# Two inverse square roots change engines in the feed-forward half: the output norm's goes to VectorE, the chain's first one to GpSimd

## The reference

```
def _layernorm(x, eps=1e-05): m = mean(x); v = var(x); return (x - m) / sqrt(v + eps)

def attn(x):                      # 16 heads of 64, softmax over 2048 keys
    ctx = softmax(q @ k.T / 8) @ v
    y = x + ctx @ Wo + bo
    return (y - mean(y)) * rsqrt(var(y) + 1e-3) * gamma + beta

def ffn(x):                       # 256 -> 768 -> 256, integer weights / 127
    return (silu(x @ wg.T) * (x @ wu.T)) @ wd.T

x = x + _layernorm(attn(_layernorm(x)))
x = x + _layernorm(ffn(_layernorm(x)))
```

## Time and profile before

| what | value |
|---|---|
| time, median of 3 runs | 2808.67 us (2808.62 to 2809.34) |
| the profiled execution's own time | 2810.7 us |
| its span | 2808.9 us |
| mean granted TensorE clock | 0.989 |
| busy share PE / DVE / ACT / POOL | 96% / 83% / 87% / 81% |
| feed-forward half | from about 2439 us to the end, some 370 us |
| one of turns 1 to 5 | 41.1 us, PE 38.8 busy, DVE 32.9, ACT 23.7, POOL 13.3 |

### The profile page before, as it was taken

One profiled execution on the slowest core, in us unless ns is written; L12 is line 12 of the kernel. 1 busy time (PEld: TensorE's weight loads), 2 busy tenths in 40 slices (PEclk: granted clock), 3 DMA queues, 4 the chain that ended last, 5 costly groups with the idle time before them and its releaser, 6 DMA issues. The chain is left out here.

```text
span 2808.9 us, 83179 instructions
## 1 busy us (share of the span) xinstructions
PE 2698.2 (96%) x34176; PEld 1727.5 (61%) x34176; DVE 2341.5 (83%) x4203; ACT 2447.0 (87%) x4760; POOL 2274.6 (81%) x1919
## 2 busy tenths in 40 slices
PE   5899999999999999899999999999999999989997
PEld 2466666666666666556666666666666666656764
DVE  4688888999998998768888889999999998678785
ACT  3799999999999999889999999999999999846553
POOL 3799999999989999789999899999999999613232
PEclk8999999999999999999999999999999999999998
DMA  3322123212211111122221222221111122321210
GB/s 101 75 56 53 40 52 75 45 41 41 41 36 39 36 40 40 39 81 58 54 46 44 53 53 41 41 42 41 41 40 40 37 42 70 99 76 46 91 53 23
DMA packets 207100, 144.89 MB, mean 52 GB/s; under 512 B 157824, under 2 KB 181632, under 8 KB 206720
## 3 DMA queue, kind: packets, MB, share of 16 engines
q1 hardware_dynamic: 206720, 139.58, 20.6%
HBM read 51.20 MB, written 37.88 MB: 32 GB/s over the span
## 5 line engine op out<-in xcount | busy, mean ns | idle before, releaser
L536 POOL TENSOR_TENSOR p_l<-p_f,p_h 128x512 f16<-128x512 f32 x1536 | 1946.2, 1295 | 92.9 <-ACT p_h L610 90.2
L663 DVE TENSOR_REDUCE mx<-ps_aux 128x1 f32<-128x512 f32 x2048 | 1349.5, 681 | 303.9 <-PE ps_aux L834 295.8
L609 ACT ACTIVATE p_f<-ps_score 128x512 f32<-128x512 f32 x2048 | 1271.7, 622 | 18.1 <-PE ps_score L863 17.9
L610 ACT ACTIVATE p_h<-ps_score 128x512 f16<-128x512 f32 x2048 | 1280.9, 627 | 0.0
L888 PEld LDWEIGHTS ps_ctx<-v_hi_one_lo,p_h 128*128 128x128 f16 x16384 | 891.4, 97 | 245.3 <-POOL p_l L536 1.2
L888 PE MATMUL ps_ctx<-v_hi_one_lo,p_h 128*128 128x65 f16 (+1 forms) x16384 | 920.8, 193 | 1.5 <-POOL p_l L536 0.9
L888 PE MATMUL ps_ctx<-v_hi_one_lo,p_l 128*128 128x65 f16 x8192 | 791.2, 192 | 0.0
L862 PE MATMUL ps_score<-q_hilo,k_hihi 128*128 128x512 f16 x2048 | 778.2, 380 | 7.4 <-ACT v_new L568 5.4
L863 PE MATMUL ps_score<-q_hi_max,k_lo_one 65*128 65x512 f16 x2048 | 780.1, 381 | 0.0
L834 PE MATMUL ps_aux<-k_hihi,q_hilo 128*128 128x512 f16 x2048 | 620.5, 382 | 21.7 <-DVE mx L663 13.7
L681 DVE TENSOR_TENSOR p_l<-p_f,p_h 128x512 f16<-128x512 f32 x512 | 536.3, 1048 | 22.6 <-ACT p_h L610 22.6
(11 more groups left out here) (174 smaller groups left out, 2163.4 us busy)
## 6 DMA issues: line engine op xcount, KB each, us to landing
v_heads<-v_new SPq DMA_DIRECT2D x64, 258.0 KB, 2.0
v_hi_one_lo<-v_heads SPq DMA_DIRECT2D x32, 516.0 KB, 6.0
heads<-ctx_n SPq DMA_DIRECT2D x128, 128.0 KB, 2.0
x_all<-heads SPq DMA_DIRECT2D x8, 2048.0 KB, 8.7
k_hihi<-hi_st SPq DMA_DIRECT2D x62, 256.0 KB, 4.4
q_hi_max<-hi_st SPq DMA_DIRECT2D x32, 256.0 KB, 3.6
k_lo_one<-lo_st SPq DMA_DIRECT2D x32, 256.0 KB, 4.3
q_hilo<-hi_st SPq DMA_DIRECT2D x31, 256.0 KB, 3.2
```

What stands on the lines that cost most here:

```text
L536: nc.gpsimd.tensor_tensor(p_l[:, r], p_f[:, r], p_h[:, r], ALU.subtract).then_inc(lo_pool, 1)
L609: nc.scalar.activation(p_f[:, r], ps_score[:, bank], ACT.Exp, scale=exp_scale)
L610: nc.scalar.activation(p_h[:, r], ps_score[:, bank], ACT.Exp, scale=exp_scale).then_inc(exp_done, 1)
L663: nc.vector.reduce_max(mx[:, blk % 2, tt, ch:ch + 1], ps_aux[:, n % SIDE], AX_X).then_inc(max_read, 1)
```

## The change

root_o moves from GpSimd, where it stood behind the first low part of the hidden slice, to VectorE, directly behind moments_o. The chain's first root moves from VectorE, where it stood behind f = 2, to GpSimd, behind the second low part (f = 1). Of this root the very first one, in the opening of the half, stays on VectorE. The root of the chain's second norm stays where it is.

```
@@ scalar
             def norm_chain(g, k, dst, src):
-                act.wait_ge(chain_root, (g * (NORMS - 1) + k) * SHIFT)
+                if k == 1:
+                    act.wait_ge(attended_root, SHIFT + g * POOL_ROOT)
+                else:
+                    act.wait_ge(chain_root, (g + 1) * SHIFT)
                 scaled(dst, src, small[3], shift, chain_normed)
...
             def norm_o(g):
-                act.wait_ge(o_root, (g + 1) * POOL_ROOT)
+                act.wait_ge(o_root, (g + 1) * SHIFT)
@@ gpsimd
-            def root_o(g):
-                pool.wait_ge(o_moments, (g + 1) * MOMENTS)
-                pool_root(nc, pool, small_o, shift_o, o_root, g * POOL_ROOT)
+            def root_attended(g):
+                pool.wait_ge(chain_moments, (g * 2 + 1) * MOMENTS)
+                pool_root(nc, pool, small, shift, attended_root, SHIFT + (g - 1) * POOL_ROOT)
...
-                    if f == 0 and g:
-                        root_o(g - 1)
+                    if f == 1 and chains(g):
+                        root_attended(g + 1)
@@ vector
             def root_chain(g, k):
-                root_here(small, shift, chain_root, (g * (NORMS - 1) + k - 1) * SHIFT)
+                if k == 1:
+                    root_here(small, shift, attended_root, 0)
+                else:
+                    root_here(small, shift, chain_root, g * SHIFT)
+
+            def root_o(g):
+                root_here(small_o, shift_o, o_root, g * SHIFT)
...
                     if f == 0 and g:
                         moments_o(g - 1)
+                        root_o(g - 1)
                     if f == 1 and chains(g):
                         moments_chain(g + 1, 1, z[1 - u])
-                    if f == 2 and chains(g):
-                        root_chain(g + 1, 1)
```

More of the change, by code:

```diff
@@ L1038, in feed_forward @@
         chain_moments = sem("chain_moments")
+        attended_root = sem("attended_root")
         chain_root = sem("chain_root")
```

## The result

| kernel | median | lowest to highest | runs |
|---|---|---|---|
| before | 2808.91 us | 2808.62 to 2810.75 | 5 |
| change | 2823.78 us | 2821.44 to 2825.46 | 5 |

The change makes the kernel slower: the ratio is 1.0051, with a 95% interval of 1.0037 to 1.0066, 14.9 us on the medians. The profiled execution has a span of 2822.0 us against 2808.9 us.

The account below looks back on a forecast made before the run. The end of the chain's root was taken to set each turn's end on PE. 5 x 2.4 + 1.4 + 1.8 + 0 = 15.2 us on 2810.7 gives 2825.9, less 2.0 for the median: 2823.9 us, range 2817 to 2829.

Parts of the forecast that it names:

- Step 1: On VectorE, root_o stands where hf 1 stood, is hit once by GpSimd's first hTl and costs 2.8 us.
- Steps 2 and 3: PE's transpose 3 waits for cTl 1, about 2 us late; ACT's hTh of f = 1 follows at 2627.03, before 2625.63.
- Step 4: GpSimd's hTl of f = 1 starts at 2627.74, its successor at 2628.86; the chain's statistics have a microsecond of slack.
- Step 5: GpSimd's fifteen root instructions take 4.26 us, so norm_attended starts 2.4 us later.
- Step 6: Everything behind norm_attended keeps its order and work, so each of turns 1 to 5 takes 2.4 us longer.
- Turn 0: No root_o here; the chain's root on GpSimd makes norm_attended 1.4 us later.
- Turn 6: An undisturbed root ahead of hf 1 makes norm_attended 1.8 us later, and PE waits for that chain's end.
- Turn 7: No chain here; its end hangs on the last hTl, so 0 was taken, with 1.85 us as upward bound.
- A: Rival: root_o isn't hit or hTl 1 isn't late; some 8 to 11 us in sum, 2818; chance 0.10.
- B: Rival: PE returns from its wait at transpose 3 at 1.2 GHz; 8 us more, 2832; chance 0.08.
- C: Rival: VectorE's list, not norm_attended, sets the turn's end; 9.3 us faster, 2799.4; chance 0.05.
- D: Rival: silu 4 isn't what hf 4 waited for, so no change within noise; 2810 to 2814; chance 0.05.

Follow-up runs that it names:

- e5: The change, with norm_attended moved on ACT from ahead of to behind the silu, high parts and hTh of f = 4: 2813.2 us.
- e6: The kernel before, with norm_attended moved behind f = 4 on ACT and the first residual behind the low parts of f = 5 on VectorE: 2801.8 us.
- e3: The change, with the output's root on VectorE moved from f = 0 to behind the low part of f = 3: 2817.0 us.
- e2: The change with root_o back on GpSimd behind f = 0, so only the chain's first root is moved: 2829.1 us.
- e9: The kernel before, with SyncE issuing the load of the next attention output ahead of the last residual's wait and store: 2809.0 us, ratio 0.9998.
- e1: The kernel before with only the output's root moved to VectorE behind its statistics: 2819.8 us.
- e4: The change, with the chain's root on GpSimd ahead of the second low part instead of behind it: 2816.2 us.

## Why the prediction was right, point by point

The forecast was 2823.9 us and the median is 2823.78. That it fits to 0.1 us is luck: the five runs of the change lie 4.0 us apart, two terms were mis-sized in opposite directions (turns 0 and 6 below), and for the profiled execution alone the sum gives 2825.9, against 2823.77 measured. What was right beyond luck is the mechanism of turns 1 to 5, step by step:

- **What bounds.** The root's end sets the turn's end over norm_attended, silu 4 and hf 4. Shown by e5, where only the position of norm_attended changes, and from the other side by e6.
- **Step 1** (root_o costs 2.8 us, hit once): 2.77 us, one instruction of 1.05 us.
- **Steps 2 and 3** (transpose 3 about 2 us late, hTh of f = 1 behind it): the wait is 1.80 us. Transpose 3 starts 11.04 us behind the turn's first ps_g (2630.93 less 2619.89); the prediction had 11.08 (2625.76 less 2614.68).
- **Step 4** (hTl 1 at 5.5 us behind hTl 0): 5.49 us. The statistics were ready 1.0 us before it ended, the slack that was predicted.
- **Step 5** (4.26 us, norm_attended 2.4 us late): 4.27 and 2.34 us.
- **Step 6** (the turn takes 2.4 us longer): 2.34 us, five times: 11.7 us for 12.0.
- **Turn 0** was mis-sized: +1.88 us for 1.4. The norm's lateness was right: norm_attended starts 21.70 us behind the turn's start (2507.58 less 2485.88) for 20.25, 1.45 us late, and e3, with the same root there, has +1.43 for the turn. The term left out was the clock. In the change PE came back from its wait of 2.17 us at transpose 7 (2511.64) at half the clock; in e2 the clock fell about half a microsecond behind the same wait; in e3 it stayed at 1.00. The change:

```profile
2511.60:2512.80 1.20, 1.16 (x6) 1.03 (x7) 1.20 (x1) 0.71 (x3) 1.20 (x2) 0.53 0.00 0
```

- **Turn 6** was mis-sized: +0.75 us for 1.8. norm_attended is 1.76 us late, as predicted (15.80 us behind the turn's first ps_g for 14.04), and so are the transposes of the normed tile. The missing microsecond is in the stretch behind them. Before (first row) and after (second), the 3.1 us that begin 1.9 us behind the first of those transposes:

```profile
2766.30:2769.40 3.10, 3.10 (x17) 2.18 (x16) 1.27 (x2) 0.60 (x1) 0.00 (x0) 0.50 0.00 0
```

```profile
2780.30:2783.40 3.10, 3.10 (x26) 2.55 (x25) 1.28 (x2) 0.60 (x1) 0.00 (x0) 0.83 0.00 0
```

  TensorE got its full clock back earlier after the change (0.83 over the stretch for 0.50, which is 1.0 us of work at full clock), although the wait ahead of it was longer (11.93 for 10.25 us). Turn 6 varies the same way between kernels that do the same there (37.62 us in before, 37.28 in e9), though by less, so I take this microsecond for chance and not for the change's. One profile of each kernel doesn't show it.
- **Turn 7** (nothing): 24.69 us for 24.61, +0.1.
- The turns together are 14.4 us longer, the forecast's 15.2 less 0.8. The span is 13.1 us longer, since turn 0 started 1.3 us earlier in this execution (first nTh at 2485.88, before 2487.18; 2483.9 to 2486.9 in the nine others). That stretch isn't touched by the change.
- **Rivals.** A (root_o not hit, or hTl 1 on time) is refuted by the rows. B (the clock) didn't happen in turns 1 to 5, but did in turn 0 and, where the wait is one piece, in e2 and in two turns of e3. C and D are out by e1, e4 and e5.
- Of the signs that were named, ACT's wait was to be over 2 us and is 1.99.

How the loss splits: the roots' places don't add. e1 costs 1.88 us a turn, e2 2.3 us at the full clock, both together 2.34. In both e2 and the change it is the start of the second low part that sets GpSimd's root, and it comes out at the same moment by two different holds. In e2 the low part stands behind root_o in GpSimd's list and starts 13.01 us behind the turn's first ps_g (2590.90 less 2577.89). In the change GpSimd is free, but the high part comes late, since root_o stands ahead of hf 1 on VectorE, and the low part starts at 13.03 us (2632.92 less 2619.89).

## What to carry to other kernels

With fixed instruction lists, ask of a moved piece when its result is first needed and what stands in the list behind the instruction that takes it; a whole engine's busy time fell here by 0.9 us a turn while the turn grew by 2.34 us. The cheapest cure for a late result is often the order of its taker: moving the norm behind a silu that doesn't need it took back 10.6 of 14.9 us. And once a wait is gone, look at the start of the next stage for a transfer that had been hidden: it took 2.8 us of the gain until its issue was moved ahead of a store.

## What the hardware showed that I had not expected

- **TensorE's clock after one wait.** The length of the wait doesn't decide whether the clock falls. At transpose 7 of e2 PE waits 3.74, 3.72, 4.10, 3.73 and 3.73 us in turns 1 to 5. Behind it the granted clock is 1.00 in turns 2 and 4, 0.50 at once in turns 3 and 5, and falls after a microsecond in turn 1 (0.57 from 2557.5 to 2558.5). In turn 0 the change, e2 and e3 have the same wait of 2.16 or 2.17 us there, and all three differ: half the clock at once, half of it a little later, and the full clock throughout. The pair of 1.80 and 1.24 us in each of turns 1 to 5 of the change never cost the clock. What else decides isn't settled by these runs, so such a loss can be priced (1.7 us a turn in e2) but not foretold from the wait.
- **The blocking between VectorE and GpSimd goes both ways in one breath.** In turn 3 of the change the first residual on VectorE starts beside an hTl, and GpSimd's next instruction starts beside the residual:

```profile
2642.26 2.04 DVE L1363 TENSOR_TENSOR x<-x_t,z 128x1024 f32<-128x1024 f32 x1
```

```profile
2642.07 1.16 POOL L1280 TENSOR_TENSOR hTl<-hf,hTh 128x512 f16<-128x512 f32 x1 [2.52 <-ACT hTh L1216]
2643.18 2.26 POOL L1265 TENSOR_TENSOR xn<-xn,bo_r 128x512 f32<-128x512 f32 x1
```

  The residual takes 2.04 us where an addition of that size takes 1.22, and ends at 2644.30, about 1.1 us after the hTl does; the bias addition takes 2.26 us, and the other one of the turn 1.27, so it stood still for 1.0 us, about until the residual was done. The Trainium skill (SBUF — State Buffer, "Who interferes with whom") has the first comer keep the shared ports for the whole instruction while the other stands still; the trace agrees in both directions.
